# Cross-attention scores as 48-row f32r products in pairs on two row groups

## What is computed

```python
x = x + attn(layernorm(x), Wq, Wkv, Wo, bo)
x = x + xattn(layernorm(x), ctx, ctx)          # this one
x = x + ffn(layernorm(x), ...)

def xattn(q, k, v):
    scores = einsum('bkgsd,bktd->bkgst', qh, kh) / 4      # 8 kv heads, 4 query heads on each, d = 16
    weights = softmax(scores)
    return einsum('bkgst,bktd->bkgsd', weights, vh)
```

## Time and profile before

| | |
|---|---|
| median of 3 runs | 1006.79 us |
| the profiled execution | 1010.77 us |
| its span, first to last instruction | 1008.9 us |
| mean granted TensorE clock | 0.958 of full speed |
| TensorE matmul busy | 920.2 us (91%) |
| VectorE busy | 660.9 us (66%) |
| ScalarE busy | 377.1 us (37%) |

### The profile page before, as it was taken

How to read it: one execution, slowest core, us unless ns; L and a number is a source line. 1 busy time by engine, 2 the same in 40 slices (tenths; PEclk the granted TensorE clock), 3 DMA queues, 4 the chain that set the end, 5 groups by cost and what they waited for, 6 DMA issues and landing times.

```text
span 1008.9 us, 16714 instructions
## 1 busy us (share of the span) xinstructions
PE 920.2 (91%) x6258; PEld 579.8 (57%) x6304; DVE 660.9 (66%) x1480; ACT 377.1 (37%) x731; POOL 275.5 (27%) x286
## 2 busy tenths in 40 slices
PE   5777999899999999999999999979999899999991
PEld 4435546654754764674575476455477556556561
DVE  1346846786885785787678678486442277777772
ACT  4031064256236325426524633533510134434430
POOL 4001001120530341152052044015115325444322
PEclk9799589799999999999999999999999999999995
DMA  4373202301410500340240050064052499999532
GB/s 140 76 269 85 62 4 74 95 3 42 114 37 3 151 19 3 84 127 4 69 121 24 17 139 17 1 187 170 24 207 51 151 394 346 345 331 349 138 46 31
DMA packets 97315, 114.70 MB, mean 114 GB/s; under 512 B 11606, under 2 KB 72470, under 8 KB 97232
## 3 DMA queue, kind: packets, MB, share of 16 engines
q1 hardware_dynamic: 83908, 94.42, 30.0%
q0 software_dynamic: 9872, 16.07, 7.1%
q10 hardware_dynamic: 3456, 3.15, 1.2%
HBM read 70.90 MB, written 16.88 MB: 87 GB/s over the span
## 4 chain that ended last, share of the span: by engine, by line
PE 74%; DVE 13%; ACT 5%; issue 5%; DMA 1%; POOL 1%; ACTq 0%; POOLq 0%; DVEq 0%
PE qa L1734 11%; PE qa L1583 6%; DVE mxx L1060 5%; PE qx L1521 5%; PE vb L1532 5%; PE qa L1377 4%; PE pt L1295 4%; PE qx L1463 4%; ACT arena L667 4%; PE qa L1295 4%; PE qa L1411 2%; PE qa L1550 2%; DVE mx L1028 2%; PE qx L1721 1%; PE qx L1719 1%
## 5 line engine op out<-in xcount | busy, mean ns | idle before, releaser
L1060 DVE TENSOR_REDUCE mxx<-qx 128x2 f32<-128x512 f32 x256 | 168.3, 685 | 45.8 <-PE qx L1463 42.8
L667 ACT ACTIVATE arena<-qx 128x512 f32<-128x512 f32 x256 | 146.4, 602 | 127.6 <-PE qx L1521 106.6
L667 ACT ACTIVATE arena<-qa 128x512 f32<-128x512 f32 (+2 forms) x125 | 67.2, 540 | 177.9 <-PE qa L1734 78.4
L521 POOL TENSOR_TENSOR rstd<-mv,power 128x2 f32<-128x2 f32 x24 | 17.2, 717 | 374.9 <-DVE mv L896 374.9
L1734 PE MATMUL qa<-arena 128*128 128x512 f32 x256 | 116.0, 596 | 1.1 <-ACT arena L667 1.1
L1463 PE MATMUL qx<-arena 96*128 96x256 bf16 x512 | 104.0, 293 | 13.6 <-DVE mxx L1060 9.6
L1521 PE MATMUL qx<-arena 98*128 98x512 bf16 x256 | 94.7, 392 | 7.0 <-ACT arena L667 2.9
L1532 PE MATMUL vb<-arena 128*32 128x256 f32 x1024 | 82.2, 393 | 1.6 <-ACT arena L667 0.4
L1463 PEld LDWEIGHTS qx<-arena 96*128 96x128 bf16 x512 | 46.7, 102 | 57.6 <-DVE mxx L1060 26.0
L1110 DVE RECIPROCAL rd<-va 128x192 f32<-128x192 f32 x32 | 43.4, 1357 | 46.9 <-PE va L1578 46.9
L1734 PEld LDWEIGHTS qa<-arena 128*128 128x128 f32 x256 | 46.2, 190 | 47.3 <-issue 47.3
(11 more groups left out here) (233 smaller groups left out, 1756.8 us busy)
## 6 DMA issues: line engine op xcount, KB each, us to landing
arena<-in_L_ffn_w SPq DMA_DIRECT2D x96, 512.0 KB
qs<-arena SPq DMA_DIRECT2D x24, 384.0 KB
arena<-arena SPq DMA_DIRECT2D x72, 128.0 KB, 3.3
res<-in_x SPq DMA_DIRECT2D x8, 512.0 KB, 7.0
xnd<-arena SPq DMA_DIRECT2D x8, 512.0 KB
ks<-arena SPq DMA_DIRECT2D x48, 64.0 KB, 1.9
arena<-arena SPq DMA_DIRECT2D x48, 64.0 KB
arena<-arena ACTq DMA_DIRECT2D x24, 128.0 KB, 3.6
```

The source lines that it names most:

```text
L667: nc.scalar.activation(dst, src, func, **kw).then_inc(s[signal], 1)
L1060: v_.reduce_max(mxx[:, col:col + 3:2], xbank[v % 2].rearrange("p (h n) -> p h n", h=2), AX.X).then_inc(s["x_max"], 1)
```

## The change

Each value is now split into two parts of type float32r (f32r), and a score is three products of parts: 3 x 16 = 48 rows, 50 with the two rows of the maximum. The even and the odd key-value heads (`side` 0 and 1) stand on two row groups of TensorE's array, from partition 0 and from partition 64 (`SIDE`), so that one matmul uses at most 50 rows of one half. The operands `qxs` and `kxs` become tensors of their own in float32r with half as many head slots.

Units are renumbered in pairs by `cross_unit`: unit v and v + 1 (v even) are of the two sides, and side 0 writes bank 0, side 1 bank 1. In pass 1 the pair's four matmuls are issued together at even v, alternating between sides, after one wait for the maxima of both units before. In pass 2 `xkeyed` issues both units of a pair at even v, each with its own wait, and `xweigh` follows at once; at odd v nothing is issued. The tables that place the other work are unchanged.

With the third part go two of the four DVE operations of the query split, and one operation each of ScalarE, DVE or GpSimd (POOL) for the context. The number of DMAs is the same (12 of 128 KB for the queries, 6 of 64 KB for the context in a stage). The expert homes drop from 10 to 8, as the new tensors take their room. `oh` becomes bf16, and a few small tensors move into the arena.

```diff
-XSPLIT_ROWS = 6 * XD
-EU = 10
+XSPLIT_ROWS = 3 * XD
+XROWS = XSPLIT_ROWS + SHIFT_ROWS
+SIDE = 64
+EU = 8
...
-        xp = [place(DC * S // 2, dt=BF16) for _ in range(3)]
-        kr = place(S)
-        kp = [place(S // 2, dt=BF16) for _ in range(3)]
+        xp = [place(DC * S, dt=F32R) for _ in range(2)]
+        kp = [place(S, dt=F32R) for _ in range(2)]
...
-        Q_ROWS = ((0, 0, "n_hi"), (1, 0, "n_hi"), (4, 0, "n_hi"), (2, 1, "n_mid"), (3, 1, "n_mid"), (5, 2, "n_split"))
+        Q_ROWS = ((0, 0, "n_hi"), (1, 0, "n_hi"), (2, 1, "n_split"))
...
+        def cross_unit(v):
+
+            pair, side = v // 2, v % 2
+            return side, pair // 4, pair // 2 % 2, pair % 2 ^ side
...
                     v_.tensor_copy(xp[0], pt[:]).then_inc(s["n_hi"], 1)
                     dve.wait_ge(s["n_hi"], k + 1)
-                    v_.tensor_tensor(xr, pt[:], xp[0], ALU.subtract).then_inc(s["n_rem"], 1)
-                    hold(dve, s["n_rem"], k + 1)
-                    v_.tensor_copy(xp[1], xr).then_inc(s["n_mid"], 1)
-                    dve.wait_ge(s["n_mid"], k + 1)
-                    v_.tensor_tensor(xp[2], xr, xp[1], ALU.subtract).then_inc(s["n_split"], 1)
+                    v_.tensor_tensor(xp[1], pt[:], xp[0].bitcast(F32), ALU.subtract).then_inc(s["n_split"], 1)
...
                     for v in range(XU):
-                        kv, t, half = v // 4, v // 2 % 2, v % 2
                         if v == XU // 2:
                             pe.wait_ge(s["qxs2_in"], k * 96)
-                        if v >= 2:
-                            pe.wait_ge(s["x_max"], k * XU - XU + v - 1)
-                        for h in range(2):
-                            op = mm(xbank[v % 2][:, h * S:h * S + S],
-                                    qxs[0:XSPLIT_ROWS, query_at(kv * 4 + half * 2 + h), t * P:t * P + P],
-                                    kxs[1 - k % 2][0:XSPLIT_ROWS, kv, :], start=True, stop=True)
-                        op.then_inc(s["xs_unit"], 1)
+                        if v % 2 == 0:
+                            if v >= 2:
+                                pe.wait_ge(s["x_max"], k * XU - XU + v)
+                            for h in range(2):
+                                for side in range(2):
+                                    _, c, t, hh = cross_unit(v + side)
+                                    rows = slice(side * SIDE, side * SIDE + XSPLIT_ROWS)
+                                    op = mm(xbank[side][:, h * S:h * S + S],
+                                            qxs[rows, query_at(c, hh * 2 + h), t * P:t * P + P],
+                                            kxs[1 - k % 2][rows, c, :], start=True, stop=True,
+                                            tile_position=(side * SIDE, 0))
+                                    if h == 1:
+                                        op.then_inc(s["xs_unit"], 1)
...
                 def xkeyed(v):
 
-                    kv, t, half = v // 4, v // 2 % 2, v % 2
-                    if v >= 2:
-                        pe.wait_ge(s["xe_ready"], k * XU - XU + v - 1)
-                    h = query_at(kv * 4 + half * 2)
-                    mm(xbank[v % 2], kxs[1 - k % 2][0:XSPLIT_ROWS + SHIFT_ROWS, kv, t * P:t * P + P],
-                       qxs[0:XSPLIT_ROWS + SHIFT_ROWS, h:h + 3:2, :], start=True, stop=True).then_inc(s["xst_unit"], 1)
+                    for side in range(2):
+                        _, c, t, hh = cross_unit(v + side)
+                        if v >= 2:
+                            pe.wait_ge(s["xe_ready"], k * XU - XU + v + side - 1)
+                        rows = slice(side * SIDE, side * SIDE + XROWS)
+                        h = query_at(c, hh * 2)
+                        mm(xbank[side], kxs[1 - k % 2][rows, c, t * P:t * P + P], qxs[rows, h:h + 3:2, :],
+                           start=True, stop=True, tile_position=(side * SIDE, 0)).then_inc(s["xst_unit"], 1)
...
                 def cross(v):
                     if v == XU // 2:
                         pe.wait_ge(s["xshift2_in"], k * 32)
-                    xkeyed(v)
-                    if v >= 3 and v % 2 == 1:
-                        xweigh((v - 3) // 2)
+                    if v % 2 == 0:
+                        xkeyed(v)
+                        if v >= 2:
+                            xweigh(v // 2 - 1)
...
-                        if v < 2:
-                            pe.wait_ge(s["x_max"], k * XU - 1 + v)
+                        if v == 0:
+                            pe.wait_ge(s["x_max"], k * XU)
```

More of the change, by code:

```diff
@@ L137, in build @@
         ks = sb("ks", [P, 2, KVH, P], F32R)
-        ARENA = 35328
+        qxs = sb("qxs", [P, XH // 2, S], F32R)
+        kxs = [sb(f"kxs{r}", [P, XKV // 2, S], F32R) for r in range(2)]
+        ARENA = 29568
         arena = sb("arena", [P, ARENA + XRING * DC * S])
@@ L501, in _ @@
                 sp.dma_start(out_rows[:, b * 2:b * 2 + 2], tokens(b)).then_inc(final_out[b], 16)
-            for e in range(7, EU):
+            for e in range(5, EU):
                 expert_in(e)
```

127 lines of the change are left out of this document (66 added, 61 removed).

## The result

| | before | after |
|---|---|---|
| median | 1006.7 us (4 runs, 1004.1 to 1013.1) | 1091.2 us (4 runs, 1088.9 to 1097.1) |
| ratio, 95% interval | | 1.083 (1.079 to 1.087) |
| span of the profiled execution | 1008.9 us | 1088.4 us |
| mean granted clock | 0.958 | 0.934 |

The forecast was 1065 us with a range of 1032 to 1097: right in sign, inside the range, 26 us short, and outside the 1046 to 1084 us that the forecast gave as its own range.

A forecast was written before the change was run, and what follows sets the result against it. TensorE was taken to bound the kernel, with VectorE 5 us behind it in pass 1. Pass 1 +49, pass 2 +3 and the clock +6 made 58 us more, for a median of 1065 us, range 1032 to 1097.

The forecast's parts named there:

- The plain pair: Pass 1 pairs with only short TensorE steps become a chain of 1.95 us, where 1.31 stood; seven in a full stage.
- L: Pass 1: time from the weight load to the end of side 0's second product, 0.51 to 0.62 us, taken as 0.55.
- The pair in which the scaling of the queries stands between the maxima: Pass 1: VectorE's query scaling now stands in the pair's chain, making it 2.81 us.
- Pass 1, +49: Pass 1 of all stages: 49 us more, as 27 in stages 3 to 7, 8, 7 and 7 in stages 1, 2, 8.
- The ends of pass 1: Units 26 to 29: lower granted clock for about 3 us in most of stages 2 to 8, 0.9 us a stage.
- The clock, +6: Term for a lower granted clock late in pass 1, partly under the waits: 6 us more.
- clock stays low in pass 1: Rival, chance 0.12: TensorE, idle a third of plain pairs, gets the lower clock in pass 1; 36 us more, 1100 us.
- Pass 2, +3: Pass 2: side-by-side gains against longer f32r loads and shape changes, +0.4 us a stage, 3 us for 8 stages.
- The stretch behind pass 2: Keys and queries keep TensorE busy there, so removed VectorE work is worth 0.
- The experts, 0: Expert part: homes cut from 10 to 8 cost 0, at worst about 13 us.
- Packing pays (1031 us): Rival, chance 0.15: sides run fully in parallel, pass 1 costs only 36 us and pass 2 gains 1.5 us a stage.
- Halving the rows of a matmul by itself gives nothing: TensorE matmuls: time goes by columns, so a gain must come from two matmuls running side by side.

The follow-up runs named there:

- e4: The changed kernel with extra matmuls without use filling TensorE's waiting time in pass 1; 1077.3 us, ratio 1.067.
- e8: The kernel before with only pass 2 issued in pairs, as the change does it; 1013.2 us, ratio 1.008.
- e9: e8 with the xkeyed products of pass 2 cut to 64 rows, still bf16; 1029.7 us, ratio 1.020.
- e1: The changed kernel with pass 1 issued unit by unit again, each unit with its own wait; 1136.3 us, ratio 1.125.
- e11: The changed kernel with pass 1's joint wait split, each side's products waiting only for their own maxima; 1075.1 us, ratio 1.065.
- e12: The changed kernel with e11's split wait and e4's filler products together, fewer fillers a pair in stages 1 and 2; 1069.3 us, ratio 1.062.
- e3: The kernel before, bf16 on the whole array, with only pass 1's joint wait for two units put in; 1038.6 us, ratio 1.031.
- e5: The kernel before, bf16 and unit by unit, with pass 1's score products cut from 96 to 64 rows; 1075.7 us, ratio 1.066.
- e10: The changed kernel with both sides' products on the first row group in both passes, so none run side by side; 1150.5 us, ratio 1.140.

## Why the prediction was right, and where it was short

**The plain pair: right.** 1.95 us forecast, 1.88 measured; L was 0.50 (weight load 563.56 to the maxima at 564.10, less 0.04), just below its 0.51 to 0.62, because the sides run fully side by side. VectorE idle 0.6 us a pair: 0.59. Pass 1 of a full stage at full clock: 38.7 forecast, 37.96 measured in stages 5 and 6. The pair in which the scaling of the queries stands between the maxima: 2.81 forecast, 2.74.

**Pass 1, +49 and most of the clock's +6: measured +63.** Its parts were right in stage 1 (+8 forecast, +8.3 measured) and at full clock (stages 5 and 6 +5.1 and +4.8, where 5.5 was forecast). The excess is in stage 2, +15.2 us where 7 was forecast, and in stage 8, +9.4 where 7 was. The ends of pass 1 were right in size: the last pair takes 4.0 to 4.4 us at the lower level in stages 3, 4, 7 and 8 and 2.53 at the higher, 6.5 us together, where 6 was forecast.

**The clock, +6: mis-sized.** e4 gave back 14 us. One place was right (the end of pass 1), but stage 2's pass 1 was taken for only a little slower, and it was at the level of 1.2 GHz for 36 us of its 49, where before it was for 10 of its 34. The measured 1091 us is nearer to the rival "clock stays low in pass 1" (1100 us) than to the forecast, but not for the rival's reason. It wanted plain pairs of 2.6 us for a third to a half of seven stages and 36 us for it; plain pairs stayed at 1.88 us in stages 3 to 7, and with the clock restored the kernel is still 7% slower. That the number lies in the range is in part luck: the range reached up to 1097 us for the sake of this rival, and what filled it was pass 2 and stage 2. The reason given for stage 1's clock, that TensorE had little to do there, doesn't fit either: it was busy 26.9 of 29.7 us at 0.60.

**Pass 2, +3: mis-sized, +15.6.** This is the step that failed most. The working let pairs with other work between gain from running side by side (up to 0.21 us a pair) and charged the rest with the exposed load and "one more change of shape", at 0.1 us each. No stage gained: the growth is 0.5 to 3.1 us in stages 1 to 7 and 3.7 in stage 8. Pairing was not free (+3.0 us over the stages in e8, 2.1 of them in stage 8), the shape is 0.6 us in stage 6 (e9), and f32r and its exposed load cost 0.5 us there beyond all that packing gives. Its ends were -27 and +15 us for eight stages, so the measured value is just outside. The stretch behind pass 2, forecast at 0, is 0.2 to 0.4 us longer in stages 1 to 6 and 2.1 in stage 7, together 3.4 us; pairing alone has 1.1 of the 2.1 (e8), the rest is open.

**The experts, 0: right**, 290.8 to 290.3 us from the end of pass 2 of stage 8. Eight homes do as well as ten, and the removed VectorE operations bought nothing that could be seen.

**Packing pays (1031 us): wrong for an instructive reason.** Its premise was true: row groups run fully in parallel, 0.23 us a pair. It failed because each pair also has to change shape there and back, which the forecast weighed as "mostly under the wait". In after that fits the plain pairs, where the chain alone gives the measured 1.88 us. But it means that undoing the wait uncovers the shape: e1 took the wait out and put a second change of shape in, and lost 45 us. My account named the joint wait as the cause; of the 84 us it is 16 (e11 against after), 8 with the clock held (e12 against e4), or 30 to 32 when it is put into before alone (e3). What stays when wait and clock are both mended (e12) is 62 us: row tiles beside full-array work, f32r loads that can't run ahead, and pass 2 (15 us of it).

**"Halving the rows of a matmul by itself gives nothing": half right.** The product itself took the same time (0.39 and 0.38 us for two), but the work around it did not: e5 has fewer rows and nothing else, and is 70 us slower.

The numbers do not add to one ledger, as the losses hide one another. Into the kernel before, the joint wait alone is +30 to 32 us, the tile shape alone in pass 1 +70, f32r on the whole array in pass 1 (with all of the changed pass 2) +28; together, with packing's gain, +84. Each of these holds what the granted clock did in that kernel.

## What to carry to other kernels

Before packing small products on row tiles, count how often the tile shape changes: in pass 1 here each round trip between a 64-row tile and the whole array cost 0.30 us with bf16 and 0.38 to 0.39 with f32r, more than running two 256-column products beside two others gave back (0.23 us). By these numbers packing can pay only where more packed products follow each other before other work of TensorE comes; no kernel here tried that. And a product that uses fewer rows than it did may leave the whole-array shape and become dearer without any packing (e5): here 96 rows ran like full-array work and 64 did not.

When a change adds a wait, price also what takes its place when the wait goes: the loss that you can see in the releasers (DVE mxx, 47 us) need not be the one that undoing it returns.

## What the runs showed that I had not expected

- Tile shape in bf16, no packing: 96 to 64 rows, +0.59 us a pair, +70 us in all, with products of nearly equal length (a mean of 293 ns before and 304 in e5, the lower clock included).
- Two row groups: in the pair above loads and products start 3 or 4 ns apart and take no longer than one side alone. Four f32r products of 256 columns take 0.50 us on two row groups, 0.73 on one. The Trainium skill, "TensorE: Matmul & The Clock Gate", Part 3, also states 4 ns between tiles; the trace agrees.
- TensorE that is busy may be at the lower level: in pass 1 of stage 8 of e10 it was busy 53.8 of 56.2 us at a granted clock of 0.50, in the same place in after 30.7 of 35.9 at 0.84. What separates the two is only that e10's products run in turn; why the clock stays low there wasn't settled. Stages with little other work paid most for it: pass 1 of stage 2 took 34.0 us before and 49.1, 54.0 and 50.9 in after, e1 and e5, and that of stage 8 26.5 us before and 62.4 in e1.
- An f32r product on the whole array costs TensorE hardly more than bf16 when its load runs beside another product (unit 0.67 against 0.65 us); where it can't run ahead, its 0.19 us stand open, against 0.11 for bf16.
